# A decoder layer on one core: new order lists for all engines, and new PSUM banks

## The reference, cut to what matters

```python
# 1: grouped attention, 32 query heads of 8 on 8 key heads, plus a memory term
q, k, v = x @ Wq.T, x @ Wk.T, x @ Wv.T
probs = softmax(einsum('bqhst', qh, kh) / sqrt(8))
a_dot = einsum('bsqhd', probs, vh)
sigma = elu(q);  a_mem = sigma @ memory / (sigma @ memory_norm)
x = layernorm(x + a_dot * (1 - w) + a_mem * w)
# 2: a fixed attention map from ctx (128 wide), applied to x
x = layernorm(x + x mixed by softmax((ctx Wq.T + bq)(ctx Wk.T + bk).T))
# 3: feed-forward 256 -> 1024 -> 256, 4-bit weights with scales, biases and rank-16 terms
x = layernorm(x + relu(x @ w_up + b_up + lora) @ w_down + b_down + lora)
```

## Time and profile before

| | |
|---|---|
| median of 3 runs | 217.09 us (217.02 to 217.85) |
| profiled execution | 216.74 us, of which the span of the instructions 214.9 us |
| PE busy | 194.3 us (90%) |
| DVE, ACT, POOL busy | 152.1, 136.1, 110.2 us |
| granted clock | 1.00 in every stretch up to 200 us, 0.93 over the last 15 us |

### The profile page before, as it was taken

How to read it: one execution, slowest core, us unless ns; L and a number is a source line. 1 busy time by engine, 2 the same in 40 slices (tenths; PEclk the granted TensorE clock), 3 DMA queues, 4 the chain that set the end, 5 groups by cost and what they waited for, 6 DMA issues and landing times.

```text
span 214.9 us, 4272 instructions
## 1 busy us (share of the span) xinstructions
PE 194.3 (90%) x1416; PEld 117.9 (55%) x1418; DVE 152.1 (71%) x278; ACT 136.1 (63%) x258; POOL 110.2 (51%) x192
## 2 busy tenths in 40 slices
...
DMA packets 15421, 12.51 MB, mean 58 GB/s; under 512 B 5944, under 2 KB 14440, under 8 KB 15112
## 3 DMA queue, kind: packets, MB, share of 16 engines
...
...
## 4 chain that ended last, share of the span: by engine, by line
PE 70%; DVE 12%; issue 6%; ACT 5%; POOL 4%; DMA 1%; POOLq 0%; DVEq 0%; ACTq 0%
PE pair L949 13%; PE pair L999 10%; PE pair L986 8%; PE pair L914 7%; PE pair L936 7%; PE pair L756 6%; DVE maxes L1130 4%; PE pair L786 4%; PE pair L971 3%; POOL y_lo L559 2%; PE pair L820 2%; DVE lora_b L1193 2%; PE pair L795 2%; PE pair L883 2%; PE pair L849 2%
## 5 line engine op out<-in xcount | busy, mean ns | idle before, releaser
L1130 DVE TENSOR_REDUCE maxes<-pair 128x4 f32<-128x1024 f32 x64 | 76.8, 1219 | 13.6 <-PE pair L914 13.0
L706 ACT ACTIVATE probs<-pair 128x1024 f32<-128x1024 f32 x64 | 63.3, 1021 | 16.1 <-PE pair L936 15.4
L949 PE MATMUL pair<-probs,V 128*32 128x512 f32 x256 | 34.1, 604 | 0.5 <-ACT probs L706 0.3
L936 PE MATMUL pair<-QT,KT 50*128 50x512 bf16 x128 | 23.6, 382 | 3.1 <-ACT probs L706 1.9
L914 PE MATMUL pair<-KT,QT 48*128 48x256 bf16 x256 | 23.7, 273 | 1.7 <-DVE maxes L1130 1.0
L459 POOL TENSOR_SCALAR rstd<-moments 128x1 f32<-128x1 f32 x24 | 4.6, 192 | 40.0 <-DVE moments L1036 39.3
L999 PE MATMUL pair<-dn_hi,y_hi 128*128 128x256 f32 x64 | 20.0, 312 | 1.2 <-DVE y_lo L1196 1.1
L914 PEld LDWEIGHTS pair<-KT,QT 48*128 48x128 bf16 x256 | 8.5, 94 | 21.7 <-issue 19.2
L986 PE MATMUL pair<-x_hi,up_hi 128*128 128x256 f32 x64 | 19.6, 307 | 0.0
L999 PE MATMUL pair<-dn_lo,y_hi 128*128 128x256 f32 x64 | 18.0, 282 | 0.0
L999 PE MATMUL pair<-dn_hi,y_lo 128*128 128x256 f32 x64 | 18.0, 281 | 0.0
...
## 6 DMA issues: line engine op xcount, KB each, us to landing
...
```

Of the source, the lines that this page charges most:

```text
L706: act.activation(probs[:, at:at + 2].rearrange("p h c -> p (h c)"), pairs[lead[stage, n] // 2][:, :], ACT.Exp, scale=SCALE)\
L936: last = pe.matmul(ps, KT[rows, b % QRING, 2 * q + j, kt * P:(kt + 1) * P], QT[rows, b % QRING, 2 * q + j, :, t * P:(t + 1) * P], start=Tr ...
L949: last = pe.matmul(ps[strip:strip + VC, :], V[:, b, kt, 4 * hh + 2 * q + j, :], probs[:, (h % RING) * 4 + 2 * j + hh], start=part == 0, st ...
L1130: dve.tensor_reduce(maxes[:, u % 2, :, j, 2 * gp:2 * gp + 2], pair.rearrange("p (h k t) -> p h k t", h=HH, k=2), X, ALU.max)\
```

## The change

No instruction is added, dropped or changed: each of the five lists holds the same tasks as before (338 words for PE, 183 for ACT, 183 for DVE, 101 for POOL, 36 for SP) in another order, and the PE list has other banks. Score tasks stand together more often: the PE list before has 89 unbroken runs of them (60 of one task, 20 of two, 8 of three, 1 of four), the new one 65 (21 of one, 27 of two, 16 of three, 1 of five). The 32 parts of P*V stood alone; now 17 do, 12 stand in pairs and 3 in a row. Cut to its core (a stretch of each list):

```diff
 PE_ORDER = """
...
-pv:2.1 dn_w:2@3 exp:5.2@0 exp:5.3@4 pv:2.2 dn_w:3@6 max:7.3@0 x1T:1@3 exp:6.0@4 xattnT:3@7 pv:2.3 exp:6.1@0
-cross:1@3 exp:6.2@4 maxT:7@2 spread:2@6 exp:6.3@0 pv:3.0@2 max:8.0@4 x2T:1@3 max:8.1@0 pv:3.1 exp:7.0@4 exp:7.1@6
-max:8.2@0 up:0.0.0@3 exp:7.2@4 up:0.0.1 exp:7.3@6 max:8.3@0 pv:3.2 max:9.0@4 max:9.1@6 pv:3.3 maxT:8@0 x1T:2@1
...
-pv:7.1 x2T:5@4 exp:15.3@6 pv:7.2 down:1.1.3 up:2.0.0@4 pv:7.3 up:2.0.1 x1T:6@5 spread:7@0 up:2.1.0@1 up:2.1.1
-up:2.2.0@4 cross:6@5 up:2.2.1 up:2.3.0@1 up:2.3.1 x1T:7@0 down:2.0.0@6 cross:7@0 x2T:6@7 down:2.0.1 down:2.0.2
...
+cross:0@1 x1T:1@0 exp:5.0@6 max:7.3@4 cross:1@0 energy:3@3 exp:5.1@6 exp:5.2@4 q:3.1 dn_w:0@1 x2T:0@4 maxT:7@5
+dn_w:1@6 mem:2.1@5 dn_w:2@7 x2T:1@0 dn_w:3@1 exp:5.3@4 pv:2.0@3 pv:2.1 pv:2.2 max:8.0@6 max:8.1@4 exp:6.0@0
+up:0.0.0@2 up:0.0.1 up:0.1.0@0 up:0.1.1 max:8.2@4 max:8.3@6 up:0.2.0@2 up:0.2.1 up:0.3.0@0 exp:6.1@4 exp:6.2@6
+up:0.3.1 maxT:8@2 pv:2.3 pv:3.0@2 max:9.0@6 exp:6.3@4 down:0.0.0@3 spread:2@1 down:0.0.1 exp:7.0@6 max:9.1@4
...
+exp:15.1@6 pv:7.1 exp:15.2@4 exp:15.3@2 up:2.0.0@1 up:2.0.1 up:2.1.0@4 up:2.1.1 up:2.2.0@5 up:2.2.1 up:2.3.0@1
+pv:7.2 pv:7.3 up:2.3.1 mem:3.1@5 spread:7@0 x1T:6@4 down:2.0.0@2 down:2.0.1 cross:6@3 down:2.0.2 down:2.0.3 x1T:7@0
...
 ACT_ORDER = """
...
-up:2.0 x1T:6 up:2.1 up:2.2 x1T:7 up:2.3 x2T:6 x2T:7 up:3.0 up:3.1 up:3.2 up:3.3
...
+exp:13.3 exp:14.0 maxT:15 exp:14.1 exp:14.2 pv:6 exp:14.3 x2T:5 exp:15.0 exp:15.1 exp:15.2 up:2.0 exp:15.3 up:2.1
+up:2.2 pv:7 up:2.3 x1T:6 x1T:7 x2T:6 x2T:7 up:3.0 up:3.1 up:3.2 up:3.3
...
 POOL_ORDER = """
-sigma:0 kv:1 dequant:0 dequant:1 dequant:2 dequant:3 lora_a:0 sigma:1 kv:2 mem:0.0 eye:0 mem:0.1 dequant:4 mem:1.0
-dequant:5 dequant:6 dequant:7 kv:3 mem:1.1 eye:1 sigma:2 lora_b:0 lora_b:1 lora_b:2 pre:0 mem:2.0 lora_b:3 mem:2.1
...
+sigma:0 mem:0.0 kv:1 dequant:0 lora_a:0 sigma:1 mem:0.1 eye:0 lora_b:0 lora_b:1 lora_b:2 mem:1.0 eye:1 lora_b:3
+dequant:1 sigma:2 dequant:2 lora_b:4 dequant:3 dequant:4 pre:0 mem:1.1 msplit:4 rs1:0 kv:2 msplit:5 eye:2 dequant:5
...
+msplit:14 rs2:5 msplit:15 rs1:6 x2b:4 rs3:3 up:2.0 up:2.1 up:2.2 mem:3.1 up:2.3 rs1:7 rs2:6 x2b:5 ln3:3 rs2:7 rs3:4
...
```

More of the change, by code:

```diff
@@ L8 @@
 PE_ORDER = """
[L9 to L18, removed]
@@ L24 @@
[L24 to L33, removed]
@@ new lines @@
+max:10.3@4 vT:3@0 down:0.1.1 max:11.0@6 mem:3.0@1 down:0.1.2 down:0.1.3 maxT:10@0 x1T:3@3 max:11.1@4 exp:8.3@6
+cross:3@3 exp:9.0@0 max:11.2@6 exp:9.1@4 pv:4.0@2 pv:4.1 exp:9.2@4 max:11.3@6 max:12.0@0 x2T:3@3 pv:4.2 exp:9.3@4
+max:12.1@6 up:1.0.0@3 up:1.0.1 up:1.1.0@4 maxT:11@5 up:1.1.1 up:1.2.0@6 up:1.2.1 up:1.3.0@3 up:1.3.1 max:12.2@4
+pv:4.3 max:12.3@6 exp:10.0@0 exp:10.1@4 down:1.0.0@3 spread:4@2 down:1.0.1 max:13.0@0 exp:10.2@6 exp:10.3@4
+down:1.0.2 down:1.0.3 maxT:12@2 max:13.1@6 exp:11.0@0 max:13.2@4 pv:5.0@3 exp:11.1@6 exp:11.2@0 x1T:4@2 pv:5.1
@@ L44 @@
[L44 to L48, removed]
@@ L61 @@
[L61 to L65, removed]
```

72 lines of the change are left out of this document (47 added, 25 removed).

## The result

The changed kernel takes 205.21 us (median of 4 runs, 204.8 to 208.79), the kernel before on the same chip 217.38 (217.02 to 217.85): a ratio of 0.943 [0.940, 0.946], 12.2 us less. The forecast was 211.5 with a range of 206.5 to 216.5, so the direction was right and the gain a little more than double the one forecast.

The account below looks back on a forecast made before the run. PE was taken to bound the kernel from 80 us on, all engines pacing each other before. 214.9 - 4.5 - 0.7 - 0.1 - 2.5 + 1.3 + 1.0 = 209.4 us of span, 211.5 as a time, range 206.5 to 216.5.

Parts of the forecast that it names:

- What bounds it: Before 80 us all engines pace each other; from 80 us on the kernel lasts as long as PE's list.
- Fewer switches: Fewer entries and exits of score and P*V runs on PE: 6.1 us, of which 4.5, 0.7 and 0.1 counted.
- The dearer price of a switch: The skill's array drain of about 0.17 us: 58 switches worth some 10 us, time about 208; not adopted.
- Half of the early switches: Before `exp:4.0`: 1.4 us of switches, counted as 0.7 (bounds 0 and 1.4), since half of PE's time there waits.
- The early part: Before `max:5.0` and `exp:4.0`: shorter lists cut PE's waits by 2.5 us (bounds 0 and 4.1).
- DVE's lead: DVE's list ahead of `max:5.0` falls from 49.0 to 44.9 us, so units start up to 4.1 us sooner.
- Close claims: Score tasks claiming a bank pair under 1.4 us after `max`, 1.2 after `exp`, filled it: 21 to 9, priced 0.
- Feed-forward in bunches: `up:0.3.0` waits 0.6 us and `down:1.0.0` 0.7 for banks that ACT holds: +1.3 us (bounds 0 and 3).
- The tail: From `exp:15.3` to `up:3`, `spread:7` comes behind all of `up:2`: 19.2 us, +1.0 (bounds 0 and 3).
- More than forecast: Rival: all 6.1 us of switches and 4.1 of DVE's lead count, no new wait: 207 us; chance 0.12.
- ACT as the bound: Rival: bunched work between `exp:5.0` and `exp:7.0`, `exp:9.0` and `exp:10.0` adds 10.7 us: 221 us; chance 0.14.
- `exp:15.3` about 6 to 8 us sooner: Sign of the forecast: `exp:15.3`, near the end of the dense part, starts about 6 to 8 us sooner.

Follow-up runs that it names:

- after_split2: Changed kernel with 19 pairs of neighbours exchanged in PE's dense part, 84 score runs instead of 65, still 9 close claims: 210.51 us, ratio 0.967.
- after_pad: Changed kernel with four extra row maxima, 3.0 us in all, in DVE's early list, which nothing waits for: 206.99 us, ratio 0.955.
- after_pairs: Changed kernel, same lists, score tasks from `exp:0.0` to `exp:4.0` held to two bank pairs instead of three at a time: 216.35 us, ratio 0.991.
- after_tight: Changed kernel with other bank pairs for `exp:1.0` to `exp:1.3`, nothing moved, 13 close claims instead of 9: 211.41 us, ratio 0.974.
- after_split: Changed kernel with 22 dense-part score tasks each moved behind the next task, 87 score runs instead of 65, 16 close claims: 214.80 us, ratio 0.985.
- before_claims: Old kernel with some twenty early PE tasks moved for fewer close claims, and one bank number changed: 218.53 us, ratio 1.005.

## Why the prediction was right or wrong

*What bounds it.* Right: PE from 80 us on, all engines together before, where the rows of after show PE at 9.8 of 10 now. The reading that the score matmuls hardly sat idle left out `exp`, the group that waited most (3.1 us).

*Fewer switches, forecast -5.3 counted of 6.1.* Right. after_split2 gives 5.4 for 4.2 priced; PE's list at the forecast's prices is 6.2 us shorter. An exit of P*V is 0.15 (1.85 for two parts, 1.00 for one), near the forecast's 0.14. One size was left out: the first feed-forward part behind any other kind costs 0.10 more than one behind its like (the earlier trace rows show it, 0.80 against the 0.70 of the list's sum), and the new list has 24 of these instead of 33, all of the difference in the dense part. That is 7.2 us of steps in all, and makes most of the 1.6 us of waits by which the ledger has the dense part shorter. The dearer price of a switch that the prediction sets beside its own, 0.17 us and 10 in all, is not borne out for score runs: entries and exits cost 0.10 in both traces. Half of the early switches were left out because "half of the PE time there waits"; by the ledger it was 23.3 of 83.4 us.

*The early part, forecast -2.5, at most -4.1, measured -7.0.* This is the step that failed. The bound of 4.1 was DVE's lead: it took the length of DVE's list for the only limit, and DVE's own idle time as given. In the traces DVE starts `max:5.0` at 59.3 instead of 70.0 us. Of these 10.7 us 5.0 are DVE work that went behind it (51.7 us before it then, 46.7 now) and 5.6 are idle time of DVE that went (18.3 and 12.7). The lead is worth what was taken (after_pad, 0.6 of each us). But the old trace had DVE idle for 4.2 us of 54 to 67, so DVE's own list could not have been the bound there, and the same windows that were read for PE would have shown it. So some 4.5 of the 7.0 come from elsewhere. What after_pairs shows is that the new order needs its third pair of banks for scores: held to two it loses 8 to 9 us, more than the 7.0. How much of the 7.0 the third pair makes is not shown: claims became closer in the same run, the new order also feeds DVE in a steadier way, and an old order with three pairs was not run. Each alone may give little and both together much. The 1.6 us ahead of `exp:0.0` lie where after_pairs changes nothing; their cause stays open (runs whose lists agree up to there reach `exp:0.0` at 42.5 to 43.8 us, so part of it can be chance).

*Close claims, forecast 0, bounds -2 and +2.* The count was right, the price of 0 was not, at least on the new lists: four more of them early cost some 3 us directly (after_tight), and seven more in the dense part came with 4.4 us beyond the switches (after_split). On the old lists one such wait only moved to the next task (before_claims), and what the others are worth there is open. The number of pairs in use, visible in the same two lists, was not looked at.

*Feed-forward in bunches, forecast +1.3.* Not seen. Waits from `exp:4.0` to `exp:15.3` are 5.5 us instead of 7.1; no single wait there exceeds 0.4, and `up:0.3.0` and `down:1.0.0`, which were to wait 0.6 and 0.7, have no idle time before them.

*The tail, forecast +1.0.* Right in mechanism, small in size: 19.9 us instead of 18.5 from `exp:15.3` to `up:3.0` (19.2 worked out); `spread:7` 8.5 us behind `exp:15.3`, 8.8 worked out. `x1T:7` waits 1.0 and `up:3.0.0` 1.3.

*The rivals.* "More than forecast" (0.12, 207) was nearest, with the wrong reason. ACT as the bound did not come: PE is at 10.0 of 10 with ACT at 8.3 at 80 to 90 us. The sign "`exp:15.3` about 6 to 8 us sooner" said that the early part was off: it came 14.3 sooner.

*The sum.* 214.9 - 6.2 - 7.0 - 1.6 + 1.9 + 0.1 is 202.1, and 0.2 more behind PE's end make the measured 202.3.
